# One kernel, two lanes: an even spread by weights replaced by written-out step orders

## The reference

```python
x = x + tanh(g_xattn[0]) * L0_xattn(ln(x), ctx)   # performer: causal linear attention, 16 heads, 32 features
x = x + tanh(g_ffn[0])   * L0_ffn(ln(x))          # self-attention of 16 heads, plus 8 linear experts, top 2
x = x + tanh(g_xattn[1]) * L1_xattn(ln(x), ctx)   # 8 heads of 64; each query keeps its 64 largest of 256 scores
x = x + tanh(g_ffn[1])   * L1_ffn(ln(x))          # 8 gated experts (top 2) and a shared one
x = x + tanh(g_xattn[2]) * L2_xattn(ln(x), ctx)   # 16 heads of 8
x = x + tanh(g_ffn[2])   * L2_ffn(ln(x))          # 8 gelu experts (top 2) and a shared one
x = x + tanh(g_xattn[3]) * L3_xattn(ln(x), ctx)   # 16 heads of 8; each query keeps its 32 largest scores
x = x + tanh(g_ffn[3])   * L3_ffn(ln(x))          # attention whose projections are mixtures of 16 experts
```

## Time and profile before

| | |
|---|---|
| median of the runs | 2963.63 us |
| span of the profiled execution, which is also its time from first to last instruction | 2962.6 us |
| busy: TensorE (PE), its weight loads, VectorE (DVE), ScalarE (ACT), GpSimd (POOL) | 85%, 62%, 70%, 47%, 31% |
| mean granted TensorE clock | 0.888 |
| blocks: first, FIRST, 1&#124;2, 3&#124;2, 3&#124;0, 1&#124;0, LAST, end | 110.2, 152.2, 162.6, 176.7, 196.9, 184.1, 125.1, 63.0 us |

### The profile page before, as it was taken

How to read it: one execution, slowest core, us unless ns; L and a number is a source line. 1 busy time by engine, 2 the same in 40 slices (tenths; PEclk the granted TensorE clock), 3 DMA queues, 4 the chain that set the end, 5 groups by cost and what they waited for, 6 DMA issues and landing times. The chain is left out here.

```text
span 2962.6 us, 41562 instructions
## 1 busy us (share of the span) xinstructions
PE 2528.0 (85%) x12585; PEld 1825.8 (62%) x12585; DVE 2068.7 (70%) x8036; ACT 1397.4 (47%) x3341; POOL 910.4 (31%) x1398
## 2 busy tenths in 40 slices
...
DMA packets 9070, 22.15 MB, mean 7 GB/s; under 512 B 642, under 2 KB 7810, under 8 KB 8066
## 3 DMA queue, kind: packets, MB, share of 16 engines
...
...
## 5 line engine op out<-in xcount | busy, mean ns | idle before, releaser
L198 DVE MATCH_REPLACE8 workQ<-top_eight,workQ 128x256 f32<-128x256 f32 x1664 | 666.3, 407 | 0.0
L200 DVE MAX8 top_eight<-workQ 128x8 f32<-128x256 f32 x1664 | 617.3, 412 | 0.8
L234 POOL TENSOR_TENSOR att_pQ<-att_pQ,top_rest 128x512 f32<-128x512 f32 x192 | 245.4, 1278 | 361.7 <-ACT top_rest L227 360.8
L507 PE MATMUL bank<-workP 128*128 128x256 f32 x1024 | 302.1, 423 | 14.1 <-POOL workP L646 4.9
L684 DVE TENSOR_REDUCE att_nmaxP<-bank 128x2 f32<-128x512 f32 x256 | 176.0, 687 | 181.4 <-PE bank L507 181.1
L567 PE MATMUL bank<-att_pTP,att_vP 128*32 128x256 f32 x1024 | 266.8, 385 | 0.6
L250 ACT ACTIVATE att_pTQ<-bank 128x512 f32<-128x512 f32 x192 | 115.4, 601 | 317.4 <-PE bank L119 317.3
L507 PEld LDWEIGHTS bank<-workP 128*128 128x128 f32 x1024 | 190.7, 205 | 102.3 <-issue 65.7
L217 ACT ACTIVATE att_pP<-bank,att_nmaxP 128x256 f32<-128x256 f32 x512 | 214.3, 476 | 37.2 <-DVE att_nmaxP L684 36.4
L646 POOL TENSOR_SCALAR workP<-workP,const 128x256 f32<-128x256 f32 x256 | 121.3, 478 | 349.6 <-PE bank L507 291.9
L250 ACT ACTIVATE att_pTP<-bank 128x512 f32<-128x512 f32 x256 | 153.5, 599 | 147.8 <-PE bank L119 146.8
...
## 6 DMA issues: line engine op xcount, KB each, us to landing
...
```

The costliest lines, as they stand in the source:

```text
L198: ins = nc.vector.match_replace(self.work[:, u % 2, j, :], eight, src, GONE)
L200: ins = nc.vector.max(eight, src)
L234: self.k.nc.gpsimd.tensor_tensor(v, v, self.rest[:, :, :], ALU.subtract).then_inc(self.p_ready, 1)
L507: mm = self.k.nc.tensor.matmul(self.banks[u % 2][:, j * T:(j + 1) * T], self.q1[:, u % self.RING, j * P:(j + 1) * P], self.kT, start=True, ...
```

## The change

The weights go, and with them `phase`. In their place each block has a string, with one letter for each step: Q takes the next step of the first chunk of the block (lane Q), P the next one of the second. Two blocks that have steps in one lane only are given None and keep their order. Nothing else changes: each step's instructions, each lane's own order, buffers and semaphores stay.

```diff
-PACE_1_2 = {"wide": (1.929, 1.4, 1.552, 1.4, 0.84), "gated": (1.4, 2.154, 1.083, 1.904, 0.246),
-            "heads2": (3.2, 1.737, 1.914, 1.549, 1.82), "gelu": (2.026, 2.169, 3.93, 1.8, 0.785)}
...
+ORDER_FIRST = (
+    "QQQPPPPPQQQQQQQPQQPQQQQPPQQPPPPQPQQPPPPQQQQQPQPPPPQQQPQQPPPQPQQQPQQQPQPPQQPQPQPQPQQPPQQQPQQPQPQQPPQQQQPQPQQPPQ"
+    "QPPQQQQPPPQQQQPQQQQPQQPPQQ")
...
-def interleaved(chunks, pace):
-
-
-    order = []
-    for n, c in enumerate(chunks):
-        steps = [(stage, s, pace[stage.name][stage.phase(s)]) for stage, s in c.steps()]
-        total, at = sum(share for _, _, share in steps), 0.0
-        for i, (stage, s, share) in enumerate(steps):
-            order.append((at / total, n, i, stage, s))
-            at += share
-    return [o[3:] for o in sorted(order, key=lambda o: o[:3])]
-
-
-def run_block(k, chunks, pace):
+def interleaved(chunks, order):
+
+    lanes = [c.steps() for c in chunks]
+    assert order is None or [order.count(letter) for letter in "QP"] == [len(lane) for lane in lanes]
+    if order is None:
+        return [step for lane in lanes for step in lane]
+    lanes = {letter: iter(lane) for letter, lane in zip("QP", lanes)}
+    return [next(lanes[letter]) for letter in order]
...
-        run_block(k, [Chunk1(k, 0), Chunk0(k, 1, None, 1)], PACE_FIRST)
+        run_block(k, [Chunk1(k, 0), Chunk0(k, 1, None, 1)], ORDER_FIRST)
```

50 lines of the change are left out of this document (25 added, 25 removed).

## The result

The changed kernel takes 2767.61 us, median of four runs (2764.62 to 2768.87), for 2963.89 us before in the same job (2962.55 to 2972.15). The ratio is 0.9335, with a 95% interval from 0.9321 to 0.935. That is 196 us less; 56.5 were forecast, and the time lies outside the range. The direction was right and the size 3.5 times too small.

The account below looks back on a forecast made before the run. No one engine bounds the kernel; TensorE's 22 to 30 us without work per block were nearly all the change could reach. Terms -6, 4x-4, 4x-4, 3x-4, 3x-1.5, -2 sum to -56.5: forecast 2907 us, range 2880 to 2945.

Parts of the forecast that it names:

- FIRST, -6: Block FIRST, once: half of VectorE's 12.34 us wait for lane Q's scores saved, -6 us; at most 12.3, possibly nothing.
- 1|2, -4: Block 1|2, four times: fewer lane Q rounds before lane P's short steps and layer norm, -4 us each; bounds -8.5 and 0.
- The signs in `gated`: Profile forecast for 1|2 and 3|2: no TensorE wait over 1.5 us in `gated`; blocks of 158.6 and 172.7 us.
- three gaps: TensorE waits in 1|2 of 1.75, 1.51 and 5.21 us; closing all three would give the bound, -8.5 us.
- 3|2, -4: Block 3|2, four times: two thirds of three gaps summing to 6.3 us saved, -4 us each; bounds -6.3 and 0.
- 3|0, -4: Block 3|0, three times: four lane Q rounds fewer up to the router's choice, -4 us each; bounds -5.8 and +1.7.
- The price of +1.7 at `perf_den`: In 3|0, five rounds before step 25 take 7.2 us against 5.48 us of idle time: 1.7 us late.
- 1|0, -1.5: Block 1|0, three times: lane P 5.8 us ahead, block end 5.9 us later, taken as -1.5 each; bounds -5.8 and +5.9.
- the tail's price: End of 1|0: four rounds and lane Q's tail after the last maximum, 5.9 us later; as slower rival, 2989 us, chance 0.13.
- LAST, -2: Block LAST, once: no lane Q rounds between steps 3 and 5 of `mixed`'s router, -2 us; bounds -6.6 and 0.
- The clock, 0 in the sum: TensorE's 1.2 GHz stretches counted as 0; rival: one goes in most blocks, -68 on top, 2839 us, chance 0.15.
- my sum of bounds (113): Lower bounds of all blocks summed: -113 us, giving 2851 us; the upper ones summed to +23, 2986 us.

Follow-up runs that it names:

- h1: Kernel before, with two lane Q rounds in 1|0 and 3|0 moved ahead of the performer's last step; 2951.55 us, ratio 0.9964.
- e1: New order in the early part of each block, the order of the kernel before behind it; 2834.67 us, before 2953.41.
- e5: Kernel before, with the new order only at the start of each block; 2951.27 us, before 2966.37 in that job.
- e6: Kernel before, with the new order only in a middle part of each block; 2913.39 us, before 2966.37 in that job.
- e3: Kernel before, with the new order only around one lane P layer norm in each block but LAST; 2904.99 us, 48 us less than before.
- w1: Kernel before, order unchanged, with unused matmuls added ahead of the turn of lane P's layer norms; 2926.04 us, ratio 0.9856.
- the pair: Two executions of block 3|0 in one follow-up kernel, same order: 5.5 us longer for 11 us more at 1.2 GHz.

## Why the prediction was wrong

**What bounds the kernel** stands: blocks in which no engine is full, and waits of TensorE and VectorE at places where the lanes cross. So does the mechanism, rounds of lane Q out of lane P's way (h1 shows it by itself), but lane Q's own waits went too, which it did not name. Two steps failed. The clock's term was put at 0: TensorE's busy time was taken as fixed (the 22 to 30 us of idle time in a block "are nearly all that it can reach"), and it fell by 93 us. And the terms of the order, with their bounds, were sized from a few waits per block: idle time fell by 103 us, much of it in waits that were not on the list. The direction was right, the size was not.

**FIRST, -6: measured -15.2.** The wait fell to 3.54 us, lower than the 5 foretold, so the lead was 8.8. With a start alone, and 8 us of lead, e1 was 1.9 us shorter and e5 0.6 longer, so the premise that lane Q sets the end, and the lead goes straight into the block's length, was wrong in both directions: it needs the order behind it, and with that the block gains more than the lead, with 17 us less at 1.2 GHz.

**1|2, -4: -8.2.** The signs in `gated` held, and the layer norm wait lost 2.9 us for 1.4. e1 and e6 put the gain in the early and middle part, where leads came that I had priced only as three gaps.

**3|2, -4: -17.2.** The term that was most too small. I took three waits of the earlier trace rows, 6.3 us, as the bound; they were 6.3 of 23 us without work. In the changed kernel idle time of TensorE in this block is 15.2 us (159.40 less 144.21), 7.9 us less, and its busy time 9.4 us less. Summed over one block, TensorE's waits for lane Q's exponentials (L217) fell from 5.9 to 2.3 us and for the copy of the turned ones (L250) from 4.3 to 2.1; of the first the list had one wait of 2.18, of the second none. e1 alone gives 13.0 of the 17.2, and e3, the part about the layer norm of `heads2`, 6.7.

**3|0, -4: -17.1.** The wait went from 4.81 to 0.27, and in h1 two rounds, 2.9 us, gave 2.4 to 3.2. But the way there was not the one foretold. VectorE before (the line behind the earlier trace rows) and after:

```profile
1464.30 0.59 DVE L275 TENSOR_SCALAR yP<-x_in,ln_mvP,ln_rstdP 128x128 f32<-128x128 f32 x2
```

```profile
1353.21 0.26 DVE L427 TENSOR_SCALAR perf_den<-bank 128x16 f32<-128x16 f32 x2 [2.37 <-PE bank L112]
...
1357.31 0.60 DVE L259 TENSOR_SCALAR yP<-x_in,ln_mvP,ln_rstdP 128x128 f32<-128x128 f32 x2 [0.82 <-POOL ln_rstdP L264]
```

The layer norm comes 2.0 us sooner after `perf_den` (4.1 for 6.1), not 4; the other 2.5 us of the wait are taken up by matmuls of lane Q that now stand ahead of the turn. The price of +1.7 at `perf_den` did not come: VectorE still waits 2.37 us for TensorE there. And e6 shows another 6.8 in the middle of the block, where the prediction named nothing: `mixed`'s waits, 2.45 us at L1482 and 1.82 at L1407 in each 3|0, were in TensorE's list of waits and not in the sum.

**1|0, -1.5: -9.0.** Two steps failed. The wait for the layer norm was to lose 1.6 to 2.6 us and lost 1.25. From `perf_den` (1644.47) to the scaled layer norm (L275 below) VectorE took 6.06 us, and now takes 3.95, 2.1 less: two rounds less, with the power on GpSimd, 0.82 us, laid open as in h1. `wide_rden` is not in the way here, as it stands three rounds ahead of `perf_den`; but its eight matmuls (1.0 us), which stood on TensorE right before this wait, are now issued well ahead, so the wait begins sooner.

```profile
1650.53 0.58 DVE L275 TENSOR_SCALAR yP<-x_in,ln_mvP,ln_rstdP 128x128 f32<-128x128 f32 x2
```

And the tail's price did not come. VectorE at the end of the block, against the earlier trace rows:

```profile
1579.05 0.69 DVE L666 TENSOR_REDUCE att_nmaxP<-bank 128x2 f32<-128x512 f32 x1 [0.35 <-PE bank L489]
...
1583.98 0.74 DVE L184 MAX8 top_eight<-workQ 128x8 f32<-128x256 f32 x2
...
1595.52 0.48 DVE L987 SCALAR_TENSOR_TENSOR x<-moe_accP,tanh_g,x_in 128x256 f32<-128x256 f32 x1
...
1597.13 0.48 DVE L830 SCALAR_TENSOR_TENSOR x<-bank,tanh_g,x 128x256 f32<-128x256 f32 x1 [1.12 <-PE bank L763]
```

The last sum ends 18.6 us after the last maximum began, 1.8 later than the 16.8 before, not 5.9: lane Q's tail after its last round (1583.98 plus 1.44) took 12.2 us, where 1|2 had shown 16.2 with `gelu` beside it. And it is hardly exposed: lane P's own way from the start of its last maximum to the end of its sum into x (L987) takes 17.0 us, so both lanes end within 2 us of each other.

**LAST, -2: -0.1.** A miss of its own: TensorE idles 7 us less in waits of 1.5 us and more, and 5 us more in shorter ones. VectorE's 435 instructions took 3.3 us more (108.90 for 105.57), most of it in `mixed`'s four products, before and after:

```profile
L1407 DVE TENSOR_TENSOR workP<-mix_wb,att_pTP 128x512 f32<-128x512 f32 x4 | 3.2, 848 | 0.0
```

```profile
L1385 DVE TENSOR_TENSOR workP<-mix_wb,att_pTP 128x512 f32<-128x512 f32 x4 | 5.4, 1382 | 0.0
```

After, the last of them takes 0.68 us with no instruction of GpSimd beside it; the other three, 1.34 to 1.76 us, all overlap one. Before, one took 1.36 us and overlapped one, three took 0.68. An overlap doesn't always lengthen them, as one of these three has one too. That the order's gain went into this is not tested.

**The clock, 0 in the sum.** It was named as a rival (-68 on top) with 0.15, on the ground that the gaps only get shorter. They did get short enough: 664 to 437 us at 1.2 GHz, a sign of being wrong that the prediction had named. At the prices measured (0.18 from w1, a lower end; 0.32 from the 22 executions of the kernel before; 0.49 from the pair) these 227 us are worth 41, 73 or 111 of the 196. The remainder, 85 to 155 us, is the order at an equal clock, by the middle price some 123 us, an estimate that carries a slope seen over 63 us at 1.2 GHz on to 227. By it both failed steps are of one size: the clock gave 73 for 0, and the order 67 more than 56.5. The order alone would then lie just beyond my sum of bounds (113). The exact shares stay open, since the low clock comes with the same waits that the order closes.

**The range.** Its lower end stood on bounds worked out from the waits on my list, and a list that is not complete bounds nothing. The bound from the windows, 22 to 30 us of idle time in sixteen blocks, would have been some 380 us, and that without the clock.
